# A vision tower layer on one NeuronCore: GpSimd weighs states in pairs, one decay ahead of silu, layers first on ScalarE, routing further apart

## The reference

```
h = window_attention(x)             # 8 heads of 8, windows of 8 x 8, 2D rope, projection
h = h + mamba(layernorm(h))         # rmsnorm, in_proj to 128 + 128, conv of 4 taps, silu,
                                    # delta = softplus(x W + b), dA = exp(delta A), 16 states:
                                    # state = dA * state + x delta B;  y = sum_n state * C
                                    # y = (y + D x) * z-gate, out_proj, + residual
h = h + moe(layernorm(h))           # router of 6 experts (MLP, softmax), top 2, softmax of the
                                    # two, three-layer experts of 64, weighted sum
```

## Time and profile before

| | us |
|---|---|
| median of 3 runs | 1745.86 (1740.89 to 1767.95) |
| the profiled execution, own time | 1745.44 |
| its span, first to last instruction | 1743.6 |
| mean granted TensorE clock | 0.862 of full speed |

### The profile page before, as it was taken

How to read it: one execution, slowest core, us unless ns; L and a number is a source line. 1 busy time by engine, 2 the same in 40 slices (tenths; PEclk the granted TensorE clock), 3 DMA queues, 4 the chain that set the end, 5 groups by cost and what they waited for, 6 DMA issues and landing times. The chain is left out here.

```text
span 1743.6 us, 27128 instructions
## 1 busy us (share of the span) xinstructions
PE 1285.7 (74%) x8651; PEld 603.4 (35%) x8724; DVE 1252.1 (72%) x1451; ACT 992.2 (57%) x1861; POOL 1090.3 (63%) x1475
## 2 busy tenths in 40 slices
PE   2765858696878868696868778686968777676665
PEld 1532515252433425152523425252524324131221
DVE  1112577797978777787968787787879787979851
ACT  2224647657574757556575757576575747564521
POOL 2013476776776676766776676767667666867630
PEclk9966979898988989798988989898889889878765
DMA  2003577786857777667767687777768676878820
GB/s 70 2 15 85 149 214 195 189 223 168 229 157 212 180 209 202 198 192 176 214 168 213 165 220 199 195 196 192 202 167 227 160 210 196 232 208 244 233 61 7
DMA packets 215206, 303.84 MB, mean 174 GB/s; under 512 B 79436, under 2 KB 79640, under 8 KB 214936
## 3 DMA queue, kind: packets, MB, share of 16 engines
q1 hardware_dynamic: 215064, 302.10, 63.9%
HBM read 274.75 MB, written 20.97 MB: 170 GB/s over the span
## 5 line engine op out<-in xcount | busy, mean ns | idle before, releaser
L1263 POOL TENSOR_TENSOR hc<-hs,c_rep 128x512 f32<-128x512 f32 x512 | 650.1, 1272 | 316.4 <-DVE hs L1043 315.1
L1043 DVE TENSOR_TENSOR_SCAN hs<-bank,state,xd 128x512 f32<-128x512 f32 x512 | 644.4, 1270 | 100.4 <-issue 93.8
L789 ACT ACTIVATE bank<-dl,a_neg 128x512 f32<-128x512 f32 x512 | 350.7, 687 | 336.1 <-DVE hs L1043 327.3
L1033 DVE TENSOR_TENSOR xd<-xd,bank 128x1024 f32<-128x1024 f32 x256 | 305.9, 1195 | 37.7 <-DMA xd<-xdel_rows 30.7
L555 PE MATMUL bank<-q_diag,k_heads 128*128 128x128 f32 x1024 | 191.4, 312 | 3.4 <-ACT top_row L782 3.2
L555 PEld LDWEIGHTS bank<-q_diag,k_heads 128*128 128x128 f32 x1024 | 166.2, 200 | 56.7 <-issue 42.8
L450 PE MATMUL bank<-hc,wts 128*32 128x512 f32 x1024 | 161.8, 693 | 5.1 <-POOL hc L1263 3.6
L1063 DVE TENSOR_REDUCE neg_max<-bank 128x8 f32<-128x512 f32 x128 | 85.7, 675 | 108.0 <-PE bank L543 108.0
L543 PE MATMUL bank<-k_heads,q_diag 64*64 64x512 f32 x512 | 94.5, 815 | 83.2 <-DMA q_diag<-rot 54.0
L716 PE MATMUL bank<-e,wts 64*64 64x512 f32 x384 | 79.5, 906 | 71.2 <-ACT e L971 71.2
L440 PE MATMUL bank<-top_sel,zeros 128*128 128x512 bf16 x439 | 128.8, 413 | 3.8 <-issue 0.7
(11 more groups left out here) (167 smaller groups left out, 2147.4 us busy)
## 6 DMA issues: line engine op xcount, KB each, us to landing
xd<-xdel_rows SPq DMA_DIRECT2D x512, 256.0 KB, 4.5
dl<-delta_rows SPq DMA_DIRECT2D x512, 256.0 KB, 4.2
delta_rows<-delta SPq DMA_DIRECT2D x16, 512.0 KB, 4.6
xdel_rows<-xdel SPq DMA_DIRECT2D x16, 512.0 KB, 3.0
xin<-in_x_dram SPq DMA_DIRECT2D x32, 128.0 KB, 2.7
q_diag<-rot SPq DMA_DIRECT2D x64, 64.0 KB
out_dram<-res SPq DMA_DIRECT2D x256, 16.0 KB
k_heads<-rot SPq DMA_DIRECT2D x128, 16.0 KB
```

The source lines that it names most:

```text
L789: act.activation(decay_ps[n % 2][:, :], dl[:, n % 4, :], ACT.Exp, scale=a_neg[:, g:g + 1])\
L1033: dve.tensor_tensor(pair, pair, b_ps[:, :].unsqueeze(1).to_broadcast([128, 2, BAND]), ALU.mult)\
L1043: dve.tensor_tensor_scan(hs[:, n % 4, :], decay_ps[n % 2][:, :], xd[:, n % 8, :], state[:, g:g + 1], ALU.mult, ALU.add).then_inc(scanned.s ...
L1263: pool.tensor_tensor(hc[:, n % 8, :], hs[:, n % 4, :], c_rep[:, BAND * h:BAND * h + BAND], ALU.mult)\
```

## The change

- `weigh` runs in odd slots only, on two slots of `hs` and `hc` at once (128 x 1024), and signals once per pair; those who wait (`scan`, `collect`, `rep`) count pairs. A pair starts when its second scan is done.
- The decay of slot 10 (EARLY) goes to PSUM bank 5 and is made on ACT in slot 7, ahead of silu, instead of in slot 8. PE's keys wait for scan 10.
- On ACT `layers` and the routing part stand first in the slot, ahead of the decay.
- Routing steps are further apart: 17 to 18, 18 to 20, 19 to 21, 20 to 23; the copy of the weights goes from DVE (slot 21) to POOL (slot 23); the turn to slot 24, at the end of PE's slot; the spread weights to slots 25 to 30, DVE's products to 26 to 31, layer three to 28, 30, 32; the output's transposes and copy one slot on.
- Norm statistics of chunk c+2 move two or three slots on, C of the second band and SP's stores one; the fillers and the slots of SOFT change.

```diff
-FILLERS = {6: 2, 7: 4, 8: 5, 11: 5, 16: 1, 23: 6, 24: 1, 25: 3, 26: 3, 29: 2}
-SOFT = (12, 15, 16, 17, 18, 19, 20, 21)
+FILLERS = {10: 1, 11: 3, 13: 2, 14: 4, 16: 2, 17: 1, 22: 2, 23: 6, 24: 4, 25: 2, 26: 2}
+SOFT = (12, 15, 16, 17, 19, 20, 21, 22)
+EARLY = 10
...
+        def decay_bank(n):
+            return psum[5] if n == EARLY else decay_ps[n % 2]
...
 SP:   keep(c + 1, 0) slot 20 -> 21; keep(c + 1, 1) slot 22 -> 23
...
 PE collect:
-                    pe.wait_ge(weighted.sem, weighted.at(k, n + 1))
+                    pe.wait_ge(weighted.sem, weighted.at(k, n // 2 + 1))
 PE keys_queries:
                 if names[0] == "k":
+                    if has(k - 3):
+                        pe.wait_ge(scanned.sem, scanned.at(k - 3, EARLY + 1))
 PE:   second slot 0 -> 1; wT slot 22 -> 24 (turn_weights, last in the slot)
-                for e, slot in enumerate((26, 28, 30)):
+                for e, slot in enumerate((28, 30, 32)):
-                if n == SLOTS + 1:
+                if n == SLOTS + 2:
-                if 23 <= n < 23 + 2 * EP:
+                if 25 <= n < 25 + 2 * EP:
...
 ACT decay:
-                if n > 1 or past(k - 1):
+                if n == EARLY:
+                    if has(k + 2):
+                        act.wait_ge(A["P6"].drained, A["P6"].empty(k + 2))
+                elif n == EARLY + 2:
+                    act.wait_ge(scanned.sem, scanned.at(k, n - 3))
+                elif n > 1 or past(k - 1):
                     act.wait_ge(scanned.sem, scanned.at(k, n - 1))
 ACT normalize: slots 23, 25, 28 -> 26, 28, 30; rep c1 slot 1 -> 2
 ACT body:
                     k, s = attention_at(c, n)
+                    if has(c - 1):
+                        layers(c - 1, n)
+                        route(c - 1, n)
                     far = ahead(c, n, 2)
-                    if far:
+                    if far and far[1] != EARLY:
                         decay(*far)
                     if has(k):
                         values_out(k, s)
+                    if has(c) and n == EARLY - 3:
+                        decay(c, EARLY)
                     if has(c):
                         second(c, odd, n)
                     if has(c - 1):
-                        layers(c - 1, n)
                         experts(c - 1, n)
...
 DVE scan:
-                    dve.wait_ge(weighted.sem, weighted.at(k, n - 3))
+                    dve.wait_ge(weighted.sem, weighted.at(k, (n - 4) // 2 + 1))
 DVE normalize: slots 20, 24 -> 22, 27; route: 17, 18, 20 -> 18, 20, 23
-                if 24 <= n < 24 + 2 * EP:
+                if 26 <= n < 26 + 2 * EP:
-                if n == 21:
-                    dve.tensor_copy(w_parts[:, :, 0, :], rt[:, 13, :, :]).then_inc(done.sem, 1)
...
 POOL weigh (body: if has(c) and n % 2):
-                pool.tensor_tensor(hc[:, n % 8, :], hs[:, n % 4, :], c_rep[:, BAND * h:BAND * h + BAND], ALU.mult)\
+                two = hs[:, (n - 1) % 4:(n - 1) % 4 + 2, :]
+                pool.tensor_tensor(hc[:, (n - 1) % 8:(n - 1) % 8 + 2, :], two,
+                                   c_rep[:, BAND * h:BAND * h + BAND].unsqueeze(1).to_broadcast([128, 2, BAND]), ALU.mult)\
                     .then_inc(weighted.sem, 1)
 POOL normalize: slots 22, 26, 29 -> 25, 29, 31; route: 17, 18, 19, 20 -> 18, 20, 21, 23
+                if n == 23:
+                    pool.wait_ge(done.sem, done.at(k, 9))
+                    pool.tensor_copy(w_parts[:, :, 0, :], rt[:, 13, :, :]).then_inc(done.sem, 1)
```

More of the change, by code:

```diff
@@ L615, in second @@
             def second(k, q, n):
-                if n == 0:
+                if n == 1:
                     if past(k - 2):
@@ L651, in experts @@
                     last.then_inc(use.filled, 1)
[L652 to L659, removed]
                 if n == 25:
@@ L674, in experts, with turn_weights @@
                     last.then_inc(use.filled, 1)
+            def turn_weights(k, n):
+                if n == 24:
+                    use = F["wT"]
+                    fill(use, k)
+                    pe.wait_ge(route_pool.sem, route_pool.at(k, 11))
+                    for i in range(4):
+                        last = pe.transpose(use.bank[0:4 * E, 128 * i:128 * i + 128],
+                                            w_parts[:, 2 * i:2 * i + 2, :, :].bitcast(F32), ident)
+                    last.then_inc(use.filled, 1)
             def weights(k, n, before, chunk):
-                if 23 <= n < 23 + 2 * EP:
-                    j = PAIRED[n - 23]
+                if 25 <= n < 25 + 2 * EP:
+                    j = PAIRED[n - 25]
                     use = W[f"wb_{j}"]
                     fill(use, k)
-                    if n == 23:
+                    if n == 25:
                         pe.wait_ge(before.drained, before.empty(chunk))
@@ L944, in experts, with route @@
                     act.activation(rh[:, :], use.bank[0:2 * RH, :], ACT.Relu, bias=rb1_2[:, :]).then_inc(use.drained, 1)
+                if n == 24:
+                    use = F["wT"]
+                    act.wait_ge(use.filled, use.full(k))
+                    copy(wT[0:4 * E, :], use.bank[0:4 * E, :]).then_inc(use.drained, 1)
+                if n == SLOTS + 1:
+                    use = F["outT"]
+                    act.wait_ge(use.filled, use.full(k))
+                    copy(outT[:, :], use.bank[:, :]).then_inc(use.drained, 1)
+            def route(k, n):
                 if n == 16:
@@ L1262, in weigh @@
                     pool.wait_ge(y_quads.sem, y_quads.at(k, n // 4 - 1))
-                pool.tensor_tensor(hc[:, n % 8, :], hs[:, n % 4, :], c_rep[:, BAND * h:BAND * h + BAND], ALU.mult)\
+                two = hs[:, (n - 1) % 4:(n - 1) % 4 + 2, :]
+                pool.tensor_tensor(hc[:, (n - 1) % 8:(n - 1) % 8 + 2, :], two,
+                                   c_rep[:, BAND * h:BAND * h + BAND].unsqueeze(1).to_broadcast([128, 2, BAND]), ALU.mult)\
                     .then_inc(weighted.sem, 1)
-                if n % 2:
-                    g, last = group(n - 1), hs[:, (n - 1) % 4:(n - 1) % 4 + 2, BAND - 1]
-                    pair = state[:, g:g + 5:4]
-                    if h == 0:
-                        pool.tensor_copy(pair, last).then_inc(stated.sem, 1)
-                    else:
-                        pool.tensor_tensor(pair, last, col("keep")[:, k + 1:k + 2].to_broadcast([128, 2]),
-                                           ALU.mult).then_inc(stated.sem, 1)
+                last, pair = two[:, :, BAND - 1], state[:, g:g + 5:4]
+                if h == 0:
+                    pool.tensor_copy(pair, last).then_inc(stated.sem, 1)
+                else:
+                    pool.tensor_tensor(pair, last, col("keep")[:, k + 1:k + 2].to_broadcast([128, 2]),
+                                       ALU.mult).then_inc(stated.sem, 1)
             def attend(k, s):
@@ L1379, in body @@
                     k, s = attention_at(c, n)
-                    if has(c):
+                    if has(c) and n % 2:
                         weigh(c, n)
```

73 lines of the change are left out of this document (32 added, 41 removed).

## The result

The changed kernel took 1786.86 us in the median of 4 runs (1783.63 to 1792.97) against 1745.19: a ratio of 1.0238, 95% interval 1.0205 to 1.0270. It is slower by some 41 us. My range (1693 to 1796) holds it; my likeliest case, 1750 and no change, was not what happened. The profiled execution took 1786.13 us, with a span of 1784.2.

A forecast was written before the change was run, and what follows sets the result against it. No engine full; a round is 78 us of VectorE work and 17 of waits from three chains. 95.41 + 1.25 - 3.65 + 3.75 + 0.95 = 97.7 against 97.3 us a round, giving 1750 us; range 1693 to 1796.

The forecast's parts named there:

- rival 2: Slots 6 to 8 without fillers: clock falls behind silu, 2.6 us a round, plus 1.3 at slot 25; 1801 us, chance 0.20.
- (e): Slots 0 to 6: slot 6 fillers go, c1 and output transposes move behind collect(7); -0.85 us together, bounds 0 and -1.5.
- (f): Scan 19 to scan 26: wait gone, gate work moved later, cast on POOL; 21.56 us becomes 17.9, -3.65.
- (a): Pair products: hidden elsewhere, but slot 13's key addition stands behind the pair, making xd 21 and queries 1.2 us later.
- (c): Layers first on ScalarE: the 1.71 us wait goes; decay 19, some 2.3 us later, costs 0.
- (d): Routing one slot on: the 3.24 us wait vanishes without gain; four route operations behind S0's maximum add 0.9.
- (g): Scan 26 to next scan 0: moved work 1.85, later weights 0.7, wb_2 1.2; +3.75 us, bounds 1.85 and 5.
- (i): PE's clock: a loss of 1.9 us a round is halved to 0.95; bounds 0 and 3.8.
- (b): Decay 10 ahead of silu: the 3.89 us wait comes back as about 1.5, 0.6 and 1.2; value 0, bounds 0 and -0.65.
- rival 3: ScalarE: decay 19 behind h2_0 and decay 21 behind h2_1 come late, 2.3 us a round; 1780 us, chance 0.08.
- The base: The round length before the change: 97.3 us, the mean of two rounds of 99.20 and 95.41 us.
- Rival 1: Fillers at slots 13, 14, 16, 17, 22 to 26 keep PE's full clock; 3.05 us a round faster, 1705 us, chance 0.30.

## Why the prediction was right or wrong

**Right in its range, wrong in the sum.** I forecast 1750 us, 0.4 us more a round, and gave "slower" 0.25. It was 1786.86, and 2.4 more a round. That 1796 as the upper end holds it is luck: that end came from rival 2, whose 2.6 us a round behind silu were 1.0. By the table the sum missed 2.0 us a round, 26 us in 13 rounds. Up to scan 13 I was 2.1 too low (e) and in (f) 1.1 too low; I was 0.4 too high in (a, c, d) and 0.9 too high in (g, i). The two rounds without attention and the ends of the run make the other 11. Behind this stand three costs that the sum had at nothing: the collision in slot 23 (1.8), the order around C's copy (1.5) and the low clock behind silu (1.0).

**(f), the collision.** My step took 0.5 off for the cast and added 0.4 for a route step, as if the short VectorE instructions kept their 0.16 to 0.2 us wherever they stood. The addition in slot 23 took 1.95, 1.79 more in 14 of 16 rounds, because a pair product of GpSimd is in flight. (f) came out at -2.51 instead of -3.65. The trace of before had the sign: the comparison of routing in slot 17 (L1158) took 1.02 us (0.21 in slot 18 of after, L1180, where no GpSimd instruction is in flight in 13 of 16 chunks), and I had counted it inside "four operations, 1.3 us" without asking why so small a thing should last that long. Taking the collision away, with the wait at TensorE for the weights, gave 41 us. This is as much as the whole difference between the kernels, but not its whole account: the order in slot 13 gave 32 and C's copy 20 more, and against these losses stand the change's gains, layers first above all.

**(a)** Right: +1.09 on the keys' chain where I gave +1.2, and the pair is 2.36, not 2.45. Scans were not held back by pairs elsewhere: the wait ahead of scan 5 in after is there with single products too (0.28 us in the mean), and fell away when C's product was moved.

**(b)** Right: 0, shown alone on the kernel before. The wait split up into three as the step had it (1.5, 0.6 and 1.2 forecast; 1.60, 0.88 and 1.14 in the mean of that run; 1.60, 1.63 and 1.28 in the round of after, where the granted clock stood at 0.50 from 996.8 to 998.1, ahead of the second).

**(c)** Right in direction, -1.7 forecast; when alone, -2.3 in its stretch and -1.6 over the round. Decay 19 behind h2_0 (rival 3) cost nothing that the runs show.

**(d)** Right together with (a): +2.1 forecast from scan 13 to 19, +1.73 measured. Not as the step had it, though: VectorE did not run straight into the wait for xd, but first 2.94 us into that for decay 18. ScalarE comes to this decay 3.4 us behind the start of scan 17, behind expert layers and routing (4.0 before), so in both kernels ScalarE's work of slot 16 leads to the wait at this place. With the xd wait mended this one is left. The comparison became 0.8 shorter by meeting no product.

**(e)** Wrong: -0.5 forecast from scan 0 to 6, +0.77 measured. I had counted PE's work from slot 30 to 4 and forgotten that the transposes of slot 2 fill the bank which C's copy empties. The run with C's product moved back gives 1.54 us a round for that order, and with it the stretch is 13.90 against 14.74 before, the side that I had forecast. From scan 6 to 13 it was -0.35 forecast and +0.50 measured. Without fillers silu did come 0.35 sooner, but the clock fell behind it, which costs 1.0; I had that in rival 2 alone.

**(g) and (i).** From scan 26 to the next 0 it was 17.65 forecast and 16.65 measured. The wait for wb_2 is there (1.02 against my 1.2), the one ahead of the first product is not in this round. (g) was too high: 16.70 forecast at the full clock, against 15.75 in the run with routing first and 15.8 in the shortest rounds of after. (i) had 0.95 for the clock, and 0.9 lie between 15.75 and 16.65. That the change halves a loss of 1.9 was my estimate, and no run shows it: in this stretch the granted clock was at 0.50 for 3.3 us a round in before and for 4.4 in after. In before, rounds of 95.4 and of 99.2 us take turns in the main, as I had read it, with 12.9 and 17.0 in this stretch and 0.50 for none and for 7.0 to 7.3 us of it.

**The base** was sound. The 97.3 from two neighbours is 97.07 in the mean of the twelve rounds behind the first; the mean over 13 is 96.38 only because the first round is short, 88.1 us, and it is short after as well (89.8).

**Rival 2** named the side on which it ended, and only a part of the cause. PE idled 4.41 us ahead of d0 (4.4 forecast) and the granted clock fell to 0.51 over d0, one of my own signs that the prediction is wrong. It costs 1.0 us a round instead of 2.6. Rival 1 did not happen in after, though the run with routing first has full clock from slot 24 on.

**The two rounds without attention** were to gain 2 and lost 6. The single-product run gives 3.0 of it back in the second of them; the rest I did not take apart.

## What to carry to other kernels

Joining two instructions of one engine into a longer one saved 0.18 us here (2.36 against twice 1.27), but it doubled the wait of what met it (the addition took 1.95 us against 0.90). Two things did: what stood behind it in its own queue (the keys' sum, 1.09 us later, and through it a full DMA queue), and instructions of a neighbour engine that did not end before it. With both out of its way the longer instruction was the better one, by 18 us. Before joining, look for tiny instructions with long durations in the trace: they can mark collisions, as the 1.02 us of the comparison in before did (0.21 with nothing in flight), and there their length was what was left of the other engine's instruction, not their own. And the longest wait of a bound engine is not the most valuable one: 3.89 us in every round were worth nothing, an order inside slot 13 was worth 2.3 in after and 1.5 in before.

## What the runs showed of the hardware that was not expected

In these runs a VectorE instruction of certain kinds that started while a GpSimd TENSOR_TENSOR was in flight did not finish before it. Worked out from the traces, for chunks 0 to 15, by whether a GpSimd instruction was in flight when the VectorE one started (medians in us, cases in brackets):

| VectorE instruction | kernel | none in flight | one in flight | its end behind GpSimd's |
|---|---|---|---|---|
| TENSOR_TENSOR of two SBUF tiles, 128x48, L1158 | before | 0.21 (1) | 1.02 (15) | 0.07 |
| SCALAR_TENSOR_TENSOR of two SBUF tiles, 128x8, L1165 | before | 0.17 (13) | 0.64 (3) | 0.03 |
| CAST, SBUF to SBUF, 128x48, L1178 | before | 0.17 (2) | 0.57 (14) | 0.05 |
| TENSOR_SCALAR, SBUF to SBUF, 128x8, L1191 | after | 0.16 (2) | 1.95 (14) | 0.03 |
| TENSOR_TENSOR of two SBUF tiles, 128x48, L1197 | after | 0.19 (13) | 2.2 to 2.28 (3) | 0.07 |

In these rows the length is what is left of the other engine's instruction and says nothing of the instruction's own. A larger one took longer as well: xdel (TENSOR_SCALAR, SBUF to SBUF, 128x1024, L1108) takes 0.69 us, and 0.88 in the median of the 15 chunks of before in which it met one, 1.69 at the most; it ended 0.55 behind GpSimd's. Others kept their durations. Scans took 1.28 us at the most, with one of GpSimd's in flight at the start of 363 of 512 before and of 292 after. In before, with none and with one in flight (medians in us), reductions took 0.20 and 0.20 (L1155) and 0.69 and 0.67 (L1063), a reciprocal 0.20 and 0.19 (L1160), and products with a PSUM operand 1.19 and 1.19 (L1033) and 0.69 and 0.69 (L1116). There is one exception among the additions: in one chunk of the kernel before, an addition (L1169) that started 0.007 us behind a GpSimd instruction of 1.29 us kept its 0.15 us. What no run here shows is what sets the two kinds apart: the reciprocal, too, goes from SBUF to SBUF, and it kept its 0.19 us where the addition and the cast did not keep theirs.
